# A four-layer transformer kernel on one core: the last net runs three slots earlier against its chunks' attention, and two routing jobs change their place

## The chip, the cores and the metric

The kernel runs on one core of a Trainium2 chip. The metric is device time in microseconds (us), from start to end of one execution. The engines named below are TensorE (PE, with its weight loads as PEld), VectorE (DVE), ScalarE (ACT), GpSimd (POOL) and SyncE (SP, which issues DMAs). Each runs its own instruction queue in order; semaphores order them against each other.

## What is computed

The input is x, 4 sequences of 1024 tokens with 128 features. Four blocks follow, each with a residual and a layer norm behind it:

```python
x = layernorm(x + L0_attn(x))   # causal attention, 16 heads of 64, 2 null keys, cosine scores, ALiBi
x = layernorm(x + L0_ffn(x))    # top-1 of 8 experts, 352 wide, silu-gated
x = layernorm(x + L1_attn(x))   # attention across the 4 sequences, 16 heads of 8, squared-distance scores
x = layernorm(x + L1_ffn(x))    # shared expert + top-2 of 16 experts, all 64 wide, silu-gated; 2x + result
```

In L1_attn the 4 sequences' tokens at one position attend to each other, with weights softmax(-|q_t - q_s|^2 / sqrt(8)). In L1_ffn a sigmoid router picks the two largest of 16 logits per token; ties go to the lower index.

## The kernel before, in words

**First stage: attention turns.** 16 turns t, one for each pair of sequence and head group of four. A turn has 18 steps s (two head pairs times nine key tiles). In each step TensorE forms scores (L635), ACT takes the exponential (L868), POOL cuts the future (L1328), TensorE multiplies by the values one step later (L662), DVE adds up the probabilities (`add`, L1095). In between, jobs that prepare turn n = t + 1 are done at fixed places: the dictionary `AT` gives each its step and "a" (before the values matmuls) or "b" (behind them), `BANK` gives each one of two PSUM banks W. The jobs' order in the dictionary is also the order in which the semaphores count them (`emptied`, `prepared`). A job waits until the previous job in its bank has been emptied (`free_for_prep`). The jobs near the change: R0 and R1 transpose the roots (L545), DVE copies them to RT (L1040); S00 to S13 spread them over the rows (L556), DVE multiplies queries and keys by them (scales, L1049, L1053); E0 and E1 transpose the ALiBi edges, and only where the head group is not "flat". In six turns (t = 5, 6, 9, 10, 13, 14) routing of the first expert layer for tokens that are already done runs alongside: XR transposes the rows (L564), XL forms the logits (L572), DVE picks the expert (`route_pick`, L237 to L245), XK forms ranks (L581 to L585), DVE turns them into row numbers (`route_place`, L1130 to L1140), POOL scatters the rows. In all six the turn prepared is flat, so E0 and E1 are absent. `masses` (L677) and `masses_turned` (L692) form the softmax sums; they use the same banks.

The expert layer (second stage) is not touched.

**Last stage.** 8 chunks of 512 tokens, each with the second attention block and the second expert net. Time is divided into periods u = -1 to 10 of nine slots j = 0 to 8 (`periods`). Each engine has a function `slot(u, j)` that lists what it does there, in order; the slots only order instructions, they have no length of their own. Attention of chunk u stands in period u, with a rest in period u + 1:

- `rows_turned` (j = 0, L1803), `project` (j = 1, L1811), differences, squares, distances, exponentials (j = 2 to 4), `shares` (DVE, j = 5, L2084 to L2089), `weigh` twice (DVE, j = 6 and 7, L2098 to L2106, which ends with `o`), `sums_turned` (j = 8, L1821), which waits for `o`;
- in period u + 1: `form` (j = 0, L1830), `joined` (DVE, L2113) and a norm, `normed_turned` (j = 2, L1840), `route` (j = 3, L1850), sigmoid, `pick_one` and `pick_other` (DVE, j = 4, L2128 to L2137 and L237 to L245), `weights` (DVE, j = 5, L2144 to L2158).

The net of chunk c has nine slots, one for each pair of experts (17 experts of 64, the last slot half full). A net slot is: `gate_up` (PE, G and U, L1870), silu (ACT, L2004), `gated` (DVE, raw = silu(G) * U, L2165), `share` (PE, M, spreads the tokens' expert weights, L1879), `shared` (DVE, hid = raw * M, L2174), and two slots later `down` (PE, Y, L1887). `share` of a slot waits for `shared` of the slot before, since both use the one buffer M. `combine` (PE, L1859) transposes the chunk's weights, ACT copies them (L1997), before the first `share`. At the end `net_home` (ACT, L2010) copies Y, `last_turned` (PE, L1898) transposes it, `ended` (DVE, L2183 and a norm's statistics) adds the residual, POOL takes the root (L183), ACT applies the norm (L194), SP stores the chunk.

Before the change the net of chunk u - 2 stands in period u with net slot i = j, so `combine(u - 2)` is in slot 0 and `last_turned`, `net_home`, `ended` and `norm1.pool_shift` of chunk u - 3 in slot 2, ACT's apply in slot 4.

`form` and `last_turned` write the same PSUM bank (Y1 and T5), `rows_turned`, `combine`, `sums_turned` and `normed_turned` the other one (T and C); `project` uses both.

Of the kernel before, what the change touches and what calls it, by code (L numbers as in the profile page):

```python
# [17 lines left out]
TT = SEQ // P  # L18
# [17 lines left out]
E0, I0 = 8, 352  # L36
# [82 lines left out]
def build(nc, a, out):  # L119
    ctx = ExitStack()  # L120
    with ctx:
# [126 lines left out]
        with ExitStack() as sc:  # L248
# [82 lines left out]
            def probs(p, jt):  # L331
# [4 lines left out]


            AT = {"P00": "0b", "P01": "0b", "P02": "1b", "P03": "2a", "N0": "3b", "T0": "4b", "V3": "4b", "P10": "5a", "P11": "5b",
# [3 lines left out]
            BANK = dict(zip(AT, (0, 1, 1, 0, 0, 0, 1, 1, 0, 1, 0, 1, 0, 0, 1, 0, 1, 1, 0, 0, 1, 0, 1, 0, 1, 0, 0, 1, 0, 0, 1)))  # L342
            PROJ = (("P00", "P01", "P02", "P03"), ("P10", "P11", "P12", "P13"))
            NORMS, TURNED, EDGE, ROOTS = ("N0", "N1"), ("T0", "T1"), ("E0", "E1"), ("R0", "R1")
            VALS = ("V0", "V1", "V2", "V3")
# [120 lines left out]
            def _(pe):  # L466
# [214 lines left out]
                def masses_turned(t, p, ahead):  # L681

                    pe.wait_ge(out_ev[0], stored(t, p, 0, 1))
                    if ahead:
                        k = PREP_BEFORE[p][1]
                        pe.wait_ge(prep_ev[1], emptied(t + 1 + p, k if k in jobs(t + 1 + p) else "V2"))
                    elif p == 0:
                        pe.wait_ge(out_ev[1], stored(t - 1, 1, 1, 3))
                    else:
                        pe.wait_ge(out_ev[1], stored(t, 0, 1, 3))  # L690
                    for u in range(4):
                        last = nc.tensor.transpose(W[1][:, u * P:(u + 1) * P], rows_d[:, u * P:(u + 1) * P], idf[:])  # L692
                    last.then_inc(out_mm, 1)
# [1008 lines left out]
        with ExitStack() as sc:  # L1702
# [62 lines left out]

            LAG = 2
            KS = NJ1 * TT

            def live(c):

                return 0 <= c < TT

            def periods(slot):

# [19 lines left out]
            def _(pe):  # L1796
# [18 lines left out]
                def sums_turned(c):  # L1815

                    pe.wait_ge(o1_ok, 2 * c + 2)
                    pe.wait_ge(qv_ok, c + 1)
                    wait_some(pe, x3_ok, c)
                    for b in range(NB):  # L1820
                        last = nc.tensor.transpose(T[:, b, :], o1[:, b, :], idf[:])  # L1821
                    last.then_inc(o_mm, 1)

                def form(c):

                    pe.wait_ge(ots_ok, c + 1)
                    pe.wait_ge(qv_ok, c + 1)
                    wait_some(pe, lg_ok, c)
                    for b in range(NB):
                        last = nc.tensor.matmul(Y1[:, b, :], ots1[:, b * P:(b + 1) * P], ow1[:], start=True, stop=True)  # L1830
                    last.then_inc(y_mm, 1)
# [21 lines left out]
                def combine(c):  # L1853

                    pe.wait_ge(w3_ok, 3 * c + 3)
                    pe.wait_ge(x3_ok, c + 1)
                    pe.wait_ge(ots_ok, min(c + 2, TT))
                    for b in range(NB):
                        last = nc.tensor.transpose(C[:, b * P:(b + 1) * P],  # L1859
                                                   w3[:, b, :, :].rearrange("p a e -> p (a e)"), idb[:])  # L1860
                    last.then_inc(c_mm, 1)
# [28 lines left out]
                def last_turned(c):  # L1890

                    pe.wait_ge(ys5_ok, c + 1)
                    pe.wait_ge(qv_ok, min(c + 4, TT))
                    pe.wait_ge(yb_ok, min(c + 3, TT))
                    pe.wait_ge(lg_ok, min(c + 2, TT))
                    wait_some(pe, x5_ok, c)
                    for b in range(NB):
                        last = nc.tensor.transpose(T5[:, b, :], ys[:, b * P:(b + 1) * P], idf[:])  # L1898
                    last.then_inc(y5_t, 1)

                def slot(u, j):

                    k = NJ1 * (u - 2) + j
                    if live(u - 2):
                        gate_up(u - 2, j)
                    if j == 0 and live(u - 1):
                        form(u - 1)
                    if j == 0 and live(u - 2):
                        combine(u - 2)
                    if 0 <= k - LAG < KS:  # L1910
                        down(k - LAG)
                    if j == 0 and live(u):
                        rows_turned(u)
                    if live(u - 2):
                        share(u - 2, j)
                    if j == 1 and live(u):
                        project(u)
                    if j == 2 and live(u - 3):
                        last_turned(u - 3)
                    if j == 2 and live(u - 1):  # L1920
                        normed_turned(u - 1)
                    if j == 3 and live(u - 1):
                        route(u - 1)
                    if j == 8 and live(u):
                        sums_turned(u)
# [5 lines left out]
            def _(act):  # L1931
# [80 lines left out]
                def slot(u, j):  # L2012

                    if j == 0 and live(u):
                        rows_normed(u)
                    if j == 2 and live(u - 3):
                        net_home(u - 3)
                    if j == 2 and live(u):
                        queries_values(u)
                    if j == 3 and live(u):  # L2020
                        squares(u)
                    if j == 4 and live(u - 3):
                        norm1.scalar_apply(act, xs, X[:, u - 3], n4(u - 3))
                    if live(u - 2):
                        silu(u - 2, j)
                    if j == 0 and live(u - 2):
                        shares_home(u - 2)
                    if j == 0 and live(u):
                        rows_home(u)
                    if j == 1 and live(u - 1):  # L2030
                        norm2.scalar_apply(act, y2, X[:, u - 1], u - 1)
                    if j == 2 and live(u - 1):
                        normed_home(u - 1)
                    if j == 4 and live(u - 1):
                        sigmoids(u - 1)
                    if j == 4 and live(u):
                        exponentials(u)
                    if j == 8 and live(u):
                        sums_home(u)
# [4 lines left out]
            def _(dve):  # L2044
# [143 lines left out]
                def slot(u, j):  # L2188

                    if j == 1 and live(u):  # L2190
                        own_rows(u)
                    if j == 2 and live(u):
                        differences(u)
                    if j == 3 and live(u):
                        distances(u)
                    if live(u - 2):
                        gated(u - 2, j)
                    if j == 0 and live(u - 1):
                        joined(u - 1)
                    if live(u - 2):  # L2200
                        shared(u - 2, j)
                    if j == 2 and live(u - 3):
                        ended(u - 3)
                    if j == 3 and live(u - 1):
                        logits(u - 1)
                    if j == 3 and live(u + 1):
                        arrive(u + 1)
                    if j == 4 and live(u - 1):
                        pick_one(u - 1)
                        pick_other(u - 1)  # L2210
                    if j == 5 and live(u - 1):
                        weights(u - 1)
                    if j == 5 and live(u):
                        shares(u)
                    if j in (6, 7) and live(u):
                        weigh(u, j - 6)
# [9 lines left out]
            def _(pool):  # L2226
# [7 lines left out]
                def slot(u, j):  # L2234

                    if j == 0 and live(u - 1):
                        norm2.pool_shift(pool, u - 1)
                    if j == 2 and live(u - 3):
                        norm1.pool_shift(pool, n4(u - 3))
                    if j == 3 and live(u + 1):  # L2240
                        norm.pool_shift(pool, n2(u + 1))
                        if u < 0:
                            get_chunk(1)
                        if live(u + 3):
                            get_chunk(u + 3)
# [78 lines left out]
```

## Time and profile before

| | us |
|---|---|
| median of 3 runs | 1722.08 (1718.21 to 1733.55) |
| the profiled execution | 1720.87, its span 1719.2 |
| the last stage, from the first gather of rows (1351.5) | 367.7 |

```profile
span 1719.2 us, 26245 instructions
## 1 busy us (share of the span) xinstructions
PE 1524.1 (89%) x8079; PEld 704.2 (41%) x8079; DVE 1022.5 (59%) x2227; ACT 767.5 (45%) x1425; POOL 533.0 (31%) x589
## 2 busy tenths in 40 slices
PE   4899999999999999999999999998399439999997
DVE  6455555655566664666555576565433267788774
PEclk8899899999999999998899999989599759999999
```

The 40 slices are 43 us each; a digit is the busy share in tenths. TensorE is busy nearly everywhere but at the start, around the change from the first to the second stage (slice 29) and between the expert layer and the last net (slices 32 and 33), where PEclk, the clock that it was granted, is also low. DVE is busiest in the last stage.

### The profile page before, as it was taken

What the parts mean: (1) busy time and instruction counts of PE and PEld (TensorE: products, weight loads), DVE (VectorE), ACT (ScalarE), POOL (GpSimd) and SP (SyncE); (2) the same over time, 40 slices, a digit from 0 to 9 for tenths busy, and PEclk for the clock granted to TensorE, in tenths of its full rate; (3) what the DMA queues carried; (4) which work ended last, traced back from release to release, by engine and by line L of the source; (5) the groups of instructions that cost most, each with busy time, mean ns of one, the idle gap of its engine ahead of it and who ended that gap; (6) DMA issues with size and microseconds to landing.
All of it is one profiled execution on the core that took longest, in us unless ns stands there. A gap on an engine that the chain in (4) does not pass through costs nothing. (4 is left out here: it accounts for less than half of the span.)

```text
span 1719.2 us, 26245 instructions
## 1 busy us (share of the span) xinstructions
PE 1524.1 (89%) x8079; PEld 704.2 (41%) x8079; DVE 1022.5 (59%) x2227; ACT 767.5 (45%) x1425; POOL 533.0 (31%) x589
## 2 busy tenths in 40 slices
PE   4899999999999999999999999998399439999997
PEld 2343344444444344443443434344277324444432
DVE  6455555655566664666555576565433267788774
ACT  3445454454544554544354454544044224444432
POOL 2043341533534444244353424432200321111000
PEclk8899899999999999998899999989599759999999
DMA  3503030320202202022020200000411100000000
GB/s 113 180 1 94 7 100 1 113 71 1 71 6 73 90 1 71 1 71 73 5 77 1 72 13 1 10 2 6 164 52 55 34 12 7 13 13 13 7 6 13
DMA packets 106708, 73.73 MB, mean 43 GB/s; under 512 B 5249, under 2 KB 100761, under 8 KB 106318
## 3 DMA queue, kind: packets, MB, share of 16 engines
q1 hardware_dynamic: 104526, 67.85, 13.1%
q0 software_dynamic: 2048, 4.20, 0.8%
q8 instruction: 71, 1.16, 0.3%
q14 instruction: 63, 0.52, 0.1%
HBM read 24.32 MB, written 47.71 MB: 42 GB/s over the span
## 5 line engine op out<-in xcount | busy, mean ns | idle before, releaser
L868 ACT ACTIVATE P<-S,keyb 128x258 f32<-128x258 f32 (+10 forms) x572 | 305.6, 592 | 401.5 <-PE S L635 294.3
L635 PE MATMUL S<-QT,KT 64*128 64x512 f32 (+5 forms) x1792 | 370.1, 494 | 7.1 <-DVE KT L1053 5.6
L1328 POOL TENSOR_SCALAR_AFFINE_SELECT P<-P 128x256 f32<-128x256 f32 (+1 forms) x256 | 162.0, 633 | 494.3 <-ACT P L868 493.6
L1095 DVE TENSOR_TENSOR Psum<-Psum,P 128x1796 f32<-128x1796 f32 (+7 forms) x256 | 283.1, 1106 | 43.6 <-POOL P L1328 30.5
L662 PE MATMUL O<-P,V 128*64 128x512 f32 (+5 forms) x1536 | 263.7, 448 | 4.5 <-POOL P L1328 3.9
L635 PEld LDWEIGHTS S<-QT,KT 64*128 64x128 f32 (+1 forms) x1792 | 161.0, 185 | 231.2 <-issue 227.3
L1305 POOL TENSOR_TENSOR rn<-nm,half 128x8 f32<-128x8 f32 (+1 forms) x120 | 220.6, 1842 | 90.7 <-DVE R L1008 47.3
L496 PE MATMUL W<-xT,wts 128*128 128x512 f32 x256 | 142.1, 650 | 10.1 <-DVE QT L1049 6.8
L662 PEld LDWEIGHTS O<-P,V 128*64 128x64 f32 (+1 forms) x1536 | 82.0, 139 | 113.9 <-issue 100.2
L1162 DVE TENSOR_TENSOR part<-W,rden 128x512 f32<-128x512 f32 x128 | 82.5, 686 | 77.1 <-PE W L711 76.1
L868 ACT ACTIVATE Psum<-S,keyb 128x1024 f32<-128x1024 f32 (+5 forms) x84 | 70.9, 911 | 125.9 <-issue 64.2
L183 POOL TENSOR_TENSOR norm_rstd<-norm_vareps,half 128x4 f32<-128x4 f32 x24 | 24.9, 1038 | 286.0 <-DVE norm_vareps L174 286.0
L802 ACT COPY qkraw<-W 128x512 f32<-128x512 f32 x128 | 75.3, 589 | 44.7 <-PE W L496 44.3
L2004 ACT ACTIVATE sg<-G 128x512 f32<-128x512 f32 (+1 forms) x72 | 42.9, 596 | 110.9 <-PE U L1870 110.8
L813 ACT ACTIVATE sq<-qkraw 128x512 f32<-128x512 f32 x128 | 80.7, 630 | 14.4
L1049 DVE SCALAR_TENSOR_TENSOR QT<-qkraw,scl,W 128x512 f32<-128x512 f32 x64 | 47.7, 745 | 58.9 <-PE W L556 58.9
L1870 PE MATMUL G<-XT,gw 128*128 128x512 f32 x144 | 81.7, 650 | 0.0
L991 DVE COPY V<-W 128x512 f32<-128x512 f32 x64 | 43.9, 687 | 61.3 <-PE W L524 61.0
L711 PE MATMUL W<-wo,OT 64*128 64x128 f32 x1024 | 73.3, 283 | 7.8 <-DVE rows_n L948 3.4
L1870 PE MATMUL U<-XT,uw 128*128 128x512 f32 x144 | 79.2, 634 | 0.0
L2165 DVE TENSOR_TENSOR raw<-sg,U 128x512 f32<-128x512 f32 (+1 forms) x72 | 49.2, 683 | 49.2 <-ACT sg L2004 49.1
L1887 PE MATMUL Y<-hid,dw 128*128 128x512 f32 x144 | 77.6, 621 | 0.0
(263 smaller groups left out, 2006.7 us busy)
## 6 DMA issues: line engine op xcount, KB each, us to landing
xg<-zero SPq DMA_DIRECT2D x16, 1216.0 KB, 10.3
yg<-zero SPq DMA_DIRECT2D x16, 1216.0 KB, 9.3
wts<-in_w_qkv SPq DMA_DIRECT2D x16, 384.0 KB, 4.1
gu<-in_gu SPq DMA_DIRECT2D x1, 2816.0 KB
xb<-xg SPq DMA_DIRECT2D x40, 64.0 KB, 1.8
yg<-yb SPq DMA_DIRECT2D x40, 64.0 KB, 1.6
X<-in_x SPq DMA_DIRECT2D x4, 512.0 KB, 5.5
wo<-in_w_out SPq DMA_DIRECT2D x16, 128.0 KB, 2.4
```

The lines of the kernel that those rows point to most:

```text
L496: nc.tensor.matmul(W[BANK[k]][:], wt[:, r, at:at + P], xT[:, n // NG % 2, NNULL + 512 * c:NNULL + 512 * c + 512], start=True, stop=True).t ...
L635: last = nc.tensor.matmul(S[hh][0:m, at + c:at + c + w], KT[d, r, p, jt * P:jt * P + m], QT[d, r, p, Q0[jt] + c:Q0[jt] + c + w], start=Tru ...
L662: last = nc.tensor.matmul(O[hh * DH:(hh + 1) * DH, lo:hi], V[0:m, r, jt, (2 * p + hh) * DH:(2 * p + hh + 1) * DH], probs(p, jt)[0:m, hh, l ...
L802: nc.scalar.copy(raw[:, c, j, :], W[BANK[k]][:]).then_inc(prep_ev[BANK[k]], 1)
L813: nc.scalar.activation(sq[:, j, :], raw[:, c, j, :], ACT.Square).then_inc(sq_ok, 1)
L868: last = nc.scalar.activation(probs(p, jt)[0:m, hh, lo:hi], S[hh][0:m, at + lo:at + hi], ACT.Exp, bias=keyb[0:m, r, col:col + 1])
L1095: nc.vector.tensor_tensor(x, x, probs(p, jt)[0:m, :, 0:NQ[jt]], ALU.add).then_inc(add_ok, 1)
L1162: nc.vector.tensor_tensor(part[:, half_, hh], W[hh][:].rearrange("p (u d) -> p u d", u=4), rden[:, p, :, 2 * half_ + hh].unsqueeze(2).broa ...
L1305: nc.gpsimd.tensor_tensor(rn[:, c, u, 0:w], nm[:, c, u, 0:w], powers[:, 0:w], ALU.pow).then_inc(rn_ok, 1)
L1328: nc.gpsimd.affine_select(own, own, [[0, 2], [1, w]], ALU.is_ge, 0.0, base=NNULL if jt == 0 else 0, channel_multiplier=-1).then_inc(cut, 1)
L1870: last = nc.tensor.matmul(o[k % 2][0:n, :], w[:, j * P:j * P + n], XT[:, c % 2, :], start=True, stop=True)
L1887: nc.tensor.matmul(Y[:], dw1[0:ROWS[j], j, :], hid[0:ROWS[j], k % 3, :], start=j == 0, stop=j == NJ1 - 1).then_inc(dn5, 1)
```

## The change

In the last stage a constant `LEAD = 3` and a function `net_slot` place the net: in slot (u, j) now stands net slot i of chunk n, with n and i the quotient and rest of 9(u - 2) + j + 3 by 9. So slots 6 to 8 of period u hold net slots 0 to 2 of chunk u - 1, and slots 0 to 5 hold net slots 3 to 8 of chunk u - 2. `combine` and its copy go with net slot 0, to (u, 6). `last_turned`, `net_home`, `ended` and `norm1.pool_shift` of chunk u - 2 go to (u, 8), ACT's apply of that norm to (u + 1, 1). On DVE `weights` of slot 5 moves ahead of that slot's `gated` and `shared`. Several waits get new operands or are new, because the buffers' users now follow each other in another order (`sums_turned` for `c_ok`, `form` for `x5_ok`, `combine` for `x2_ok`). No instruction of computation is added or removed.

In the attention turns XL moves from 14a to 10b, with bank 1 in place of 0, and XK from 15b to 14b, also with bank 1. `masses_turned` waits for the last job in its bank, which may now be XL.

```diff
-                  "R0": "11a", "S00": "12b", "S01": "12b", "S02": "13b", "S03": "13b", "XL": "14a", "E1": "14b",
-                  "R1": "15a", "XK": "15b", "S10": "16a", "S11": "16b", "S12": "18a", "S13": "18a"}
+            ... "E0": "10b", "XL": "10b",
+                  "R0": "11a", "S00": "12b", "S01": "12b", "S02": "13b", "S03": "13b", "E1": "14b", "XK": "14b",
+                  "R1": "15a", "S10": "16a", "S11": "16b", "S12": "18a", "S13": "18a"}
...
                     if ahead:
-                        k = PREP_BEFORE[p][1]
-                        pe.wait_ge(prep_ev[1], emptied(t + 1 + p, k if k in jobs(t + 1 + p) else "V2"))
+                        n = t + 1 + p
+                        k = next(j for j in ("XL", "E0", "V2") if j in jobs(n)) if p == 0 else PREP_BEFORE[p][1]
+                        pe.wait_ge(prep_ev[1], emptied(n, k))
...
+            LAG, LEAD = 2, 3
+            def net_slot(u, j):
+                return divmod(NJ1 * (u - 2) + j + LEAD, NJ1)
...
 sums_turned:
+                    wait_some(pe, c_ok, c)
 form:
+                    wait_some(pe, x5_ok, c - 1)
 combine:
-                    pe.wait_ge(ots_ok, min(c + 2, TT))
+                    pe.wait_ge(ots_ok, c + 1)
+                    pe.wait_ge(x2_ok, min(c + 2, TT))
 last_turned:
-                    pe.wait_ge(qv_ok, min(c + 4, TT))
-                    pe.wait_ge(yb_ok, min(c + 3, TT))
+                    pe.wait_ge(qv_ok, min(c + 3, TT))
+                    pe.wait_ge(yb_ok, min(c + 2, TT))
...
 TensorE, slot(u, j):
-                    k = NJ1 * (u - 2) + j
-                    if live(u - 2):
-                        gate_up(u - 2, j)
+                    n, i = net_slot(u, j)
+                    k = NJ1 * n + i
+                    if live(n):
+                        gate_up(n, i)
                     if j == 0 and live(u - 1):
                         form(u - 1)
-                    if j == 0 and live(u - 2):
-                        combine(u - 2)
+                    if i == 0 and live(n):
+                        combine(n)
                     if 0 <= k - LAG < KS:
                         down(k - LAG)
...
-                    if live(u - 2):
-                        share(u - 2, j)
+                    if live(n):
+                        share(n, i)
...
-                    if j == 2 and live(u - 3):
-                        last_turned(u - 3)
+                    if j == 8 and live(u - 2):
+                        last_turned(u - 2)
...
 ScalarE:
-                    if j == 2 and live(u - 3):
-                        net_home(u - 3)
+                    if j == 8 and live(u - 2):
+                        net_home(u - 2)
...
-                    if j == 4 and live(u - 3):
+                    if j == 1 and live(u - 3):
                         norm1.scalar_apply(act, xs, X[:, u - 3], n4(u - 3))
...
 VectorE:
+                    if j == 5 and live(u - 1):
+                        weights(u - 1)
+                    if live(n):
+                        gated(n, i)
...
-                    if j == 2 and live(u - 3):
-                        ended(u - 3)
+                    if j == 8 and live(u - 2):
+                        ended(u - 2)
...
-                    if j == 5 and live(u - 1):
-                        weights(u - 1)
...
 GpSimd:
-                    if j == 2 and live(u - 3):
-                        norm1.pool_shift(pool, n4(u - 3))
+                    if j == 8 and live(u - 2):
+                        norm1.pool_shift(pool, n4(u - 2))
```

## Rows read from the trace of the kernel before

**Rows 1.** Windows, one period each from `sums_turned`: us, busy per engine, clock, DMA

```profile
1411.36:1450.51 39.15, 34.25 (x100) 15.57 (x100) 28.68 (x77) 17.36 (x33) 6.35 (x8) 0.94 0.03 7
1450.51:1490.44 39.93, 35.71 (x107) 16.16 (x108) 31.59 (x90) 18.19 (x37) 7.53 (x10) 0.96 0.05 14
...
1568.52:1606.72 38.20, 34.03 (x108) 15.31 (x108) 31.55 (x90) 18.08 (x37) 3.68 (x6) 1.00 0.02 8
...
1646.61:1678.70 32.09, 31.73 (x96) 13.29 (x96) 21.87 (x65) 13.63 (x24) 2.42 (x4) 1.00 0.02 9
```

**Rows 2.** Waits of TensorE in the last stage: total us, times, longest

```profile
PE W L1821 <- DVE o L2106: 35.8, 8, 15.0
```

**Rows 3.** Timeline of TensorE, period 6: start, us, instruction, [idle before <- releaser]

```profile
1571.71 0.41 PE L1859 MATMUL W<-idb,w 128*51 128x128 bf16 x4
...
1581.86 0.66 PE L1898 MATMUL W<-idf,ys 128*128 128x128 f32 x4
...
1589.77 1.13 PE L1870 MATMUL G<-XT,gw 128*128 128x512 f32 x2
...
1592.86 1.13 PE L1870 MATMUL G<-XT,gw 128*128 128x512 f32 x2
...
1595.89 0.39 PE L1879 MATMUL M<-comb,sel 51*128 51x512 bf16 x1 [0.19 <-DVE hid L2174]
...
1600.76 0.39 PE L1879 MATMUL M<-comb,sel 51*128 51x512 bf16 x1 [1.71 <-DVE hid L2174]
...
1606.72 0.66 PE L1821 MATMUL W<-idf,o 128*128 128x128 f32 x4 [1.93 <-DVE o L2106]
```

**Rows 4.** Timeline of DVE, the same period

```profile
1571.85 0.69 DVE L2165 TENSOR_TENSOR raw<-sg,U 128x512 f32<-128x512 f32 x1 [2.09 <-ACT sg L2004]
...
1582.75 0.68 DVE L2183 SCALAR_TENSOR_TENSOR xs<-X,W 128x512 f32<-128x512 f32 x1
...
1590.90 0.19 DVE L2128 TENSOR_SCALAR sc<-sc 128x64 f32<-128x64 f32 x1
...
1594.43 0.68 DVE L2165 TENSOR_TENSOR raw<-sg,U 128x512 f32<-128x512 f32 x1
...
1597.65 0.20 DVE L2155 CAST w<-wt 128x68 bf16<-128x68 f32 x1
...
1606.24 0.42 DVE L2106 TENSOR_TENSOR o<-prod 128x256 f32<-128x256 f32 x1
```

**Rows 5.** Timeline at the start of the last stage, all engines

```profile
1393.79 0.59 ACT L1984 COPY XT<-W 128x512 f32<-128x512 f32 x1 [1.22 <-PE W L1840]
...
1404.59 0.22 DVE L2155 CAST w<-wt 128x68 bf16<-128x68 f32 x1
...
1410.88 0.42 DVE L2106 TENSOR_TENSOR o<-prod 128x256 f32<-128x256 f32 x1
...
1412.26 1.91 PE L1870 MATMUL G<-XT,gw 128*128 128x512 f32 x2
```

**Rows 6.** Timeline of DVE in period 8: the last pick, the last weight

```profile
1670.21 0.22 DVE L245 TENSOR_TENSOR hot<-key,top 128x64 f32<-128x64 f32 x1
...
1673.58 0.20 DVE L2155 CAST w<-wt 128x68 bf16<-128x68 f32 x1
```

**Rows 7.** Timelines of attention turns: turn 5 with routing, then turn 2 without

```profile
480.93 1.06 PE L572 MATMUL W<-rw,xtr 128*128 128x8 f32 x8
485.68 0.39 PE L545 MATMUL W<-idb,R 128*24 128x128 bf16 x4 [1.93 <-DVEq L1121]
487.42 0.19 PE L581 MATMUL W<-rhot,tri 128*128 128x32 bf16 x1 [0.55 <-DVE RT L1040]
...
488.16 0.17 DVE L1130 TENSOR_TENSOR rspot<-W,held 128x32 f32<-128x32 f32 x1
...
488.74 0.19 DVE L1140 TENSOR_REDUCE place<-rspot 128x4 uint32<-128x32 f32 x1
...
269.83 0.87 PE L662 MATMUL O<-P,V 128*64 128x386 f32 x4 [0.35 <-POOL P L1328]
272.86 0.50 PE L556 MATMUL W<-RT,selr 24*128 24x512 bf16 x1 [1.73 <-DVE RT L1040]
```

More of the change, by code:

```diff
@@ L338, in build @@
             AT = {"P00": "0b", "P01": "0b", "P02": "1b", "P03": "2a", "N0": "3b", "T0": "4b", "V3": "4b", "P10": "5a", "P11": "5b",
[3 rows of a table removed]
-            BANK = dict(zip(AT, (0, 1, 1, 0, 0, 0, 1, 1, 0, 1, 0, 1, 0, 0, 1, 0, 1, 1, 0, 0, 1, 0, 1, 0, 1, 0, 0, 1, 0, 0, 1)))
[3 rows of a table added]
+            BANK = dict(zip(AT, (0, 1, 1, 0, 0, 0, 1, 1, 0, 1, 0, 1, 0, 0, 1, 0, 1, 1, 1, 0, 0, 1, 0, 1, 1, 1, 0, 1, 0, 0, 1)))
             PROJ = (("P00", "P01", "P02", "P03"), ("P10", "P11", "P12", "P13"))
@@ L1763, in build @@
                 s4("x_ok5"), s4("m5"), s4("st_out"))
-            LAG = 2
+            LAG, LEAD = 2, 3
             KS = NJ1 * TT
@@ L2015, in slot @@
                         rows_normed(u)
-                    if j == 2 and live(u - 3):
-                        net_home(u - 3)
+                    n, i = net_slot(u, j)
+                    if j == 8 and live(u - 2):
+                        net_home(u - 2)
                     if j == 2 and live(u):
@@ L2021, in slot @@
                         squares(u)
-                    if j == 4 and live(u - 3):
+                    if j == 1 and live(u - 3):
                         norm1.scalar_apply(act, xs, X[:, u - 3], n4(u - 3))
[L2024 to L2027, printed above, removed]
+                    if live(n):
+                        silu(n, i)
+                    if i == 0 and live(n):
+                        shares_home(n)
                     if j == 0 and live(u):
@@ L2195, in slot @@
                         distances(u)
-                    if live(u - 2):
-                        gated(u - 2, j)
+                    n, i = net_slot(u, j)
+                    if j == 5 and live(u - 1):
+                        weights(u - 1)
+                    if live(n):
+                        gated(n, i)
                     if j == 0 and live(u - 1):
                         joined(u - 1)
-                    if live(u - 2):
-                        shared(u - 2, j)
-                    if j == 2 and live(u - 3):
-                        ended(u - 3)
+                    if live(n):
+                        shared(n, i)
+                    if j == 8 and live(u - 2):
+                        ended(u - 2)
                     if j == 3 and live(u - 1):
```

2 rows, old and new, of the table AT are left out of this document.

## Prediction

> **What bounds the kernel now.** I read the table of windows over the last stage first. From one period to the next (39.15, 39.93 and 38.20 us in the rows, the others like them) TensorE is busy 34 of 38.20 us at full clock, so it is the bound, with about 4 us of holes per period; DVE is busy 31.55 of them, so it is close behind [rows 1]. Period 8, which has no attention, and the net of chunk 7 behind it have no such holes: 31.73 of 32.09 us busy in period 8 [rows 1]. Then the waits: TensorE's largest in this stage is `sums_turned` (L1821), which waits for the attention's last sum `o` on DVE, 35.8 us over 8 times, once 15.0 [rows 2]. The timelines of one period show why. In slots 0 to 4 TensorE runs without a hole; a clean slot takes 1592.86 - 1589.77 = 3.09 us. In slots 5 to 8 it waits 0.19, 1.71 and 1.93 us for DVE (and once more, 0.34, by the same pattern) [rows 3]. DVE has just begun the routing picks (1590.90), then has one slot's pair of products (1594.43), the weights (to 1597.85), the shares and the two `weigh`s, and ends `o` at 1606.66: 15.76 us without a gap [rows 4]. So a period is a TensorE-bound part (slots 0 to 4) and a DVE-bound part (slots 5 to 8).
>
> At the stage's start the net has nothing to do: XT of chunk 0 is there at 1394.4, its weights at 1404.8, yet the first gate matmul of the net begins at 1412.26, at half clock, behind the attention of chunk 1, whose `o` ends at 1411.30 [rows 5]. That hole is the 15.0 us of [rows 2].
>
> **The change, part by part** (against the profiled run: span 1719.2, its time 1720.87; the median of the runs is 1.2 us above that).
>
> *Head.* Net slots 0 to 2 of chunk 0 now stand in slots 6 to 8 of period 1, before `sums_turned(1)`. Gate 0 can run at 1396; `combine`, the copy of its result and share 0 need the weights (1404.8). DVE then has the shares of chunk 1, two pairs of products and two `weigh`s; in a later period this very list takes 1606.66 - 1597.85 = 8.8 us [rows 4], so `o` is ready at 1413.6 at the earliest. TensorE is at half clock: a gate pair takes 2 x 1.71 = 3.4 us (the G row starts 1.71 before its U) [rows 5]. Share 0 ends near 1407.0, gate 1 1410.4, gate 2 1414.2, then one `down` and share 2: `sums_turned(1)` at 1415.6, against 1411.36. Bounds: 1413.6, and 1417.8 if everything up to there is at half clock. Term: +4.2 (+2.2 to +6.4).
>
> *First full period.* Before, it starts cold and takes 39.15 [rows 1]; now it is warm and ordinary, 38.20 - 0.84 (next step) = 37.4. Term: -1.8. The two `down`s that the old period lacked (slots 0 and 1) are in the ordinary period's length.
>
> *Every later period.* `combine` moves from slot 0 to 6, `last_turned` from 2 to 8, out of the part where TensorE is the bound: 0.34 + 0.50 us start to start (durations 0.41 and 0.66 overlap their successors) [rows 3]. The holes in slots 5 to 8 take them. Within those slots nothing shortens: the weights now stand ahead of pair 5, so TensorE's share 6 waits some 2.1 us longer (1597.85 - 1595.75, [rows 4]), but share 7 waited for the same DVE list anyway; DVE's list from picks to `o` is the same 15.76 us. The copy of the weights' turned result (ACT, 0.6) ends before pair 5 does. ACT's norm apply moves from slot 4 to 1, where it must fit between `rows_home` and the silu; by the timeline it does, and at slot 4 the silu waited for TensorE. The DMA issues are the same and stay behind the same signals; SP only gets each output store about three slots earlier, POOL's `pool_shift` goes from behind slot 2 to behind the gathers of slot 3, which wait for nothing there. `ended` (2.3 us, 1582.75 to 1585.1) moves to behind pair 8, queued ahead of pair 0, `joined` and the next norm; DVE idled 2.09 there [rows 4], so about 0.2 us is late, and `joined`'s result is needed four us later. Term: 5 x -0.84 = -4.2; bounds 0 and -4.2.
>
> *Tail.* From `sums_turned(7)` the old kernel needs 1719.2 - 1646.61 = 72.6 us [rows 1]. Removed: three slots, 9.3; one `combine` and one `last_turned`, 0.8; two small waits, 0.4. Added: chunk 7's `combine` now comes in slot 6 of period 8. Old: picks end at 1670.43, pair 5, weights end at 1673.78 [rows 6]; now the weights follow the picks, 1672.5 - 0.84 = 1671.7, while TensorE has ended gate 6 at about 1669.8 and has 1.3 us (`combine`, `down`) to do before share 6, which needs pair 5, ready 1.3 after the weights, 1673.0. Stall 2.1. Term: -9.3 - 0.8 - 0.4 + 2.1 = -8.4 (bounds -6.7, if half clock follows the stall, and -10.5, without it).
>
> *Clock.* Each period holds one stretch at half clock. Where it falls into slots 5 to 8 it costs nothing (38.20), where behind `o` it costs 1.7 us (39.93) [rows 1]; three periods of six pay. The holes move, and I can't tell where the stretches go: 0, bounds -5.1 and +5.1. The first G at 1412.26 is at 1.2 GHz after the 15 us hole [rows 5]. The Trainium skill ("TensorE: Matmul & The Clock Gate", Part 1) says that the array runs at half rate by default and that recent activity releases it; the trace agrees. By that rule alone fewer holes would mean fewer slow stretches, and all of them gone is the first rival below.
>
> *Routing in attention turns* (turns 5, 6, 9, 10, 13, 14; the next turn is flat, so E0 and E1 are absent). XL goes from 14a to 10b and bank 0 to 1, XK from 15b to 14b. Now R1 waits 1.93 us for DVE, whose picks are queued behind two late `add`s, and XK 0.5 more [rows 7]. Both waits vanish. But DVE is the bound there: a turn without routing shows the next wait, the spread of R1's roots behind RT, 1.73 us [rows 7]. XL's 1.0 us of matmuls now stands ahead of the scales that the late `add`s wait for, and so delays both engines alike; `route_place`, 488.93 - 488.16 = 0.77 us, comes ahead of RT on DVE, and XK's 0.3 us ahead of the spread on TensorE. The wait there becomes 1.73 + 0.77 - 0.3 = 2.2 us, and with the 0.35 us for POOL's cut, which that turn also shows, 2.55 us stand against 1.93 + 0.55 = 2.48 now [rows 7]. Term 0. Bounds: -2.5 x 6 = -14.9 if the two waits simply go; +0.77 x 6 = +4.6 if the place comes on top of what routed turns lose now. Nearest the row of the unrouted turn: 0. Queued behind XL's picks on DVE is RT of R0, for which it idles some 3 us. `masses_turned` now waits for those picks, which end before its own turn.
>
> Sum: 4.2 - 1.8 - 4.2 - 8.4 + 0 = -10.2. Profiled run 1710.7; against the median 1711.9. I say 1711.5.
>
> **The rivals.**
> - *Clock*: no slow stretch falls behind `o`: 5.1 less, 1706.5. For it: fewer holes; against: every period now has one stretch, hole or not. 0.15.
> - *Routing waits go*: R1's and XK's 2.48 us in six turns are real gain, 14.9 less, 1696.6. For it: TensorE is the bound over the turn; against: the 1.73 us wait in a turn without any routing. 0.10.
> - *The periods don't shorten*: `ended` and the norm apply, at their new places, hold up pair 0 and the silu of slot 1 as much as TensorE was relieved: terms two and three lose 5 us, 1716.5. For it: DVE's 2.3 us against 2.09 idle; against: only 0.2 is late. 0.14.
> - *Slower than before*: `form` now waits for `ended`'s first operation of the slot before (they share PSUM). That is done 2.05 us behind `o`, `form` comes at 2.27. If it came a whole `ended` later, each of seven boundaries would cost up to 2.3 us: 1711.5 + 16 = 1727.6. It decides from 1.5 us per boundary. Against: `last_turned` stands ahead of `sums_turned` and its input is copied 3 us before. 0.06, with half of it beyond 1% once clock loss is added.
>
> **How the numbers follow.** The forecast has 0.55, with its own range 1706 to 1716.5. The range is 1701 to 1719: it takes in the clock and the third rival and leaves out the routing gain and the slower case. One per cent, about what a measurement can tell here from no change, is 17.2 us. Faster by more needs the routing gain, or clock and the best bounds together: 0.12. Slower by more (over 1739): 0.03. Same: 0.85.
>
> **What would show it.** `sums_turned(1)` about 4 us later, with three gate pairs before it; periods of 37.4 us (39.1 with a slow stretch); TensorE's wait at share 6 near 2 us, and less at L1821, above all the 15.0; in period 8 a 2 us stall at share 6; no wait at R1, and about 1.9 us at the spread behind it, with routed turns as long as before. Periods that stay at 38.2, or waits at `form`, would prove steps three and five wrong; routed turns 2 us shorter, the routing step.

## The result, and the profile after

The changed kernel takes 1714.92 us (median of 15 runs, 1710.36 to 1721.04) against 1724.20 us of the kernel before (15 runs, 1717.11 to 1733.55) on the same chip: ratio 0.9949, 95% interval 0.9935 to 0.9964. That is some 9 us less, within 1%. The forecast was 10.2 less. The size is right, but two of its terms, both put at nothing, were wrong with opposite signs: one by 5 us, the other by 8 to 10, as the parts and the experiments show.

The page of the changed kernel, its span, TensorE's busy share in 40 slices and the clock granted to it:

```profile
span 1717.9 us, 26266 instructions
...
PE   4899999999999999999999999998669748989997
...
PEclk8899998998989999899989999999779958999999
```

This profiled execution took 1719.64 us, 4.7 above its median, and that of before 1720.87, 3.3 below its own. So the two spans differ by only 1.3 us, and the parts must be compared, not the spans:

| part | before | after | difference |
|---|---|---|---|
| to `masses` of turn 0 | 106.5 | 107.8 | +1.3 |
| attention turns, `masses` of turn 0 to that of turn 15 | 1076.4 | 1090.3 | +13.9 |
| from there to the last stage | 168.6 | 169.9 | +1.3 |
| last stage: head, to `sums_turned(1)` | 59.9 | 63.0 | +3.1 |
| first full period | 39.15 | 37.25 | -1.9 |
| five later periods | 196.1 | 186.2 | -9.9 |
| tail, from `sums_turned(7)` | 72.6 | 63.5 | -9.1 |

The last stage is 17.8 us shorter, and the attention turns, where the forecast expected nothing, are 13.9 longer. Of these 13.9, 5.6 lie in turns 0 to 4, whose instructions are the same in both kernels (the table by turns in experiment 4), and so can't come from the change.

Windows of the changed kernel: the head, the first full period and the last of the six, the tail; then the attention turns, and the second half of turn 6. Columns as in [rows 1]; the last three are clock, DMA share and GB/s.

```profile
1368.00:1430.95 62.95, 27.60 (x69) 15.30 (x69) 34.25 (x101) 17.41 (x39) 26.25 (x28) 0.55 0.08 21
1430.95:1468.20 37.25, 34.12 (x108) 15.14 (x108) 29.94 (x79) 16.66 (x33) 6.33 (x8) 1.00 0.03 8
...
1617.18:1654.44 37.26, 35.54 (x110) 15.50 (x108) 29.82 (x79) 18.21 (x37) 2.42 (x4) 0.95 0.02 7
1654.44:1717.90 63.46, 53.13 (x147) 20.68 (x145) 35.07 (x100) 21.05 (x39) 4.83 (x8) 0.95 0.04 13
...
107.84:1198.14 1090.30, 1035.75 (x6091) 448.90 (x6090) 646.54 (x1142) 518.76 (x917) 432.17 (x458) 0.95 0.14 41
...
546.55:582.29 35.74, 32.38 (x196) 13.97 (x195) 23.26 (x43) 13.72 (x24) 12.76 (x16) 0.90 0.01 3
```

The same two stretches of the kernel before:

```profile
106.54:1182.93 1076.39, 1022.01 (x6092) 443.87 (x6091) 647.18 (x1142) 517.70 (x917) 431.94 (x458) 0.96 0.14 41
...
538.44:571.64 33.20, 29.55 (x196) 13.35 (x195) 23.26 (x43) 13.56 (x23) 11.88 (x16) 1.00 0.01 3
```

Two things are to be read here. Every period is now 37.2 us, whether its clock is 1.00 or 0.95, where before it was 38.20 or about 39.9 [rows 1]. And half a turn with the same matmuls went from 33.20 to 35.74 us, while its clock went from 1.00 to 0.90.

The waits of TensorE in the last stage (us in total, times, longest):

```profile
PE W L1827 <- DVE o L2116: 18.7, 6, 12.8
...
PE W L1867 <- DVE w L2165: 11.8, 5, 4.9
PE W L1867 <- issue: 5.1, 3, 1.7
```

`sums_turned` (now L1827) waits 18.7 us where it waited 35.8 [rows 2]. In its place `combine` (now L1867) waits for the weights, 16.9 us in eight times (for three of them, 5.1 us, the profile names no releaser; that they are the weights too is inferred from the place).

One period of TensorE, to be read against [rows 3]; L1878 is `gate_up`:

```profile
1607.05 0.41 PE L1867 MATMUL W<-idb,w 128*51 128x128 bf16 x4 [1.71 <-DVE w L2165]
...
1608.83 2.07 PE L1878 MATMUL G<-XT,gw 128*128 128x512 f32 x2
...
1617.18 0.64 PE L1827 MATMUL W<-idf,o 128*128 128x128 f32 x4
```

And of DVE, to be read against [rows 4]: `ended` (L2193), the next pair of products (L2175), the first pick, the last weight, the last `o`:

```profile
1581.11 0.68 DVE L2193 SCALAR_TENSOR_TENSOR xs<-X,W 128x512 f32<-128x512 f32 x1
1583.36 0.68 DVE L2175 TENSOR_TENSOR raw<-sg,U 128x512 f32<-128x512 f32 x1
...
1601.24 0.20 DVE L2138 TENSOR_SCALAR sc<-sc 128x64 f32<-128x64 f32 x1 [0.16 <-ACT sc L1999]
...
1606.80 0.20 DVE L2165 CAST w<-wt 128x68 bf16<-128x68 f32 x1
...
1616.69 0.42 DVE L2116 TENSOR_TENSOR o<-prod 128x256 f32<-128x256 f32 x1
```

The three holes of 0.19, 1.71 and 1.93 us in slots 5, 6 and 8 have become one of 1.71 us in slot 6, and it stands 10 us ahead of `o`. DVE's list from picks to `o` still takes 15.87 us (15.76 before), which sets the length of slots 5 to 8. The half-clock stretch (a gate of 2.07 us in place of 1.13) lies inside them, so nothing is paid for it.

A routed attention turn of the changed kernel (turn 6), to be read against the first three of [rows 7]: R1 (L545), the first spread S10 (L556), values and scores:

```profile
566.31 0.39 PE L545 MATMUL W<-idb,R 128*24 128x128 bf16 x4
...
570.48 0.37 PE L556 MATMUL W<-RT,selr 24*128 24x512 bf16 x1 [2.42 <-DVE RT L1041]
570.78 0.97 PE L662 MATMUL O<-P,V 128*64 128x258 f32 x4
...
573.31 3.87 PE L635 MATMUL S<-QT,KT 64*128 64x512 f32 x8 [0.28 <-DVE KT L1054]
```

The waits at R1 (1.93) and XK (0.55) are gone, and one of 2.42 stands at the spread, as forecast (2.2). But behind it eight score matmuls take 3.87 us, at half clock, where the same eight of the kernel before take 2.08.

### The profile page after: what moved, and what is told of

Same layout as the page of the kernel before. It is cut to its first block and busy times, and to the rows that moved or that the text cites. A ratio compares the mean times of both kernels' runs of the same rounds, so it can differ in the third digit from the quotient of the medians.

```text
span 1717.9 us, 26266 instructions
## 1 busy us (share of the span) xinstructions
PE 1535.4 (89%) x8079; PEld 706.7 (41%) x8079; DVE 1022.7 (60%) x2227; ACT 769.2 (45%) x1425; POOL 533.1 (31%) x589
## 5 line engine op out<-in xcount | busy, mean ns | idle before, releaser
L635 PE MATMUL S<-QT,KT 64*128 64x512 f32 (+5 forms) x1792 | 378.1, 502 | 6.2 <-DVE KT L1054 4.6
L496 PE MATMUL W<-xT,wts 128*128 128x512 f32 x256 | 150.4, 685 | 8.5 <-DVE QT L1050 5.5
L1878 PE MATMUL G<-XT,gw 128*128 128x512 f32 x144 | 82.3, 655 | 0.0
L556 PE MATMUL W<-RT,selr 24*128 24x512 bf16 x128 | 49.5, 441 | 33.7 <-DVE RT L1041 29.8
L1878 PE MATMUL U<-XT,uw 128*128 128x512 f32 x144 | 76.9, 617 | 0.0
L496 PEld LDWEIGHTS W<-xT,wts 128*128 128x128 f32 x256 | 43.3, 204 | 79.5 <-issue 51.8
```

Of the source, the lines that this page charges most:

```text
L496: nc.tensor.matmul(W[BANK[k]][:], wt[:, r, at:at + P], xT[:, n // NG % 2, NNULL + 512 * c:NNULL + 512 * c + 512], start=True, stop=True).t ...
L635: last = nc.tensor.matmul(S[hh][0:m, at + c:at + c + w], KT[d, r, p, jt * P:jt * P + m], QT[d, r, p, Q0[jt] + c:Q0[jt] + c + w], start=Tru ...
L1878: last = nc.tensor.matmul(o[k % 2][0:n, :], w[:, j * P:j * P + n], XT[:, c % 2, :], start=True, stop=True)
```

## The experiments

Each was run against the kernel before on the chip that it ran on; these were three chips, with medians of the kernel before from 1722.84 to 1723.88 us. Theory H ("half clock"): the attention turns are longer only because more of them runs at 1.2 GHz. Its rival R: the routing jobs' new place costs TensorE or DVE time in itself.

**1. Only the net, only the routing.** The first leaves `AT`, `BANK` and `masses_turned` as before the change, the second changes nothing else.

> The changed kernel with the attention turns' XL and XK put back where they were. The change's profile shows the last stage 17.8 us shorter and the attention turns 15 us longer than before. Theory A (the attention turns' length is set by where the half-clock stretches fall, and the routing jobs' place has nothing to do with it): same time as the whole change, about 0.995 of the kernel before, with a last stage of about 350 us. Theory B (the routing jobs' new place costs the turns what the net gains): about 0.990, 17 us less than before, and attention turns as long as before.

Measured: 1705.43 us (1704.44 to 1706.86), ratio 0.9895 (0.9877 to 0.9913), 17.4 less than before.

> The kernel before with only the routing jobs moved. Theory A: the same time as before, 0.998 to 1.002, with S10's spread waiting 2.4 us in place of R1's 1.93 and XK's 0.55. Theory B: 8 to 15 us more than before, 1.005 to 1.009. The rival of the prediction (the two waits go): 15 us less, 0.991.

Measured: 1730.69 us (1725.13 to 1736.14), ratio 1.0047 (1.0030 to 1.0063), 7.9 more. So the net's part alone gains 1%, and the routing's part loses about half of that; the two add up to 9.5 us less, where the whole change measured 9.3. Windows, net only (the turns, then the last stage's first full period):

```profile
107.28:1186.08 1078.80, 1024.33 (x6091) 445.18 (x6090) 646.62 (x1142) 518.03 (x917) 432.56 (x458) 0.96 0.14 41
...
1417.62:1454.87 37.25, 34.12 (x108) 15.14 (x108) 29.93 (x79) 16.67 (x33) 6.34 (x8) 1.00 0.03 8
```

and routing only:

```profile
107.13:1192.16 1085.03, 1029.83 (x6091) 447.19 (x6090) 646.28 (x1142) 518.77 (x917) 430.68 (x458) 0.96 0.14 41
```

The gain lies in the last stage (350.3 us, with the periods of the whole change), the loss in the turns.

**2. Which of the two moves.** XL moves to 10b as in the change, XK stays at 15b with bank 0:

```diff
-  "XL": "10b" ... "XK": "14b", "R1": "15a"
+  "XL": "10b" ... "R1": "15a", "XK": "15b"
```

> The kernel before with XL and its picks at 10b, but XK and route_place where they were (15b, behind RT on DVE). If route_place ahead of RT is what lengthens the hole from 1.7 to 2.4 us and brings the half-clock stretches: about the time before (0.997 to 1.001), with 1.6 us of waiting at S10's spread or XK in place of 2.42. If XL's work ahead of the late adds does it: as the routing-only kernel, 1.0047.

Measured: 1733.10 us (1727.77 to 1740.07), ratio 1.0058 (1.0035 to 1.0081), 10.0 more. XL's move alone is enough to bring the whole loss. XK then waits 2.06 us itself, and the half-clock stretch comes again:

```profile
490.82 0.19 PE L581 MATMUL W<-rhot,tri 128*128 128x32 bf16 x1 [2.06 <-DVE RT L1041]
...
494.07 4.00 PE L635 MATMUL S<-QT,KT 64*128 64x512 f32 x8 [0.28 <-DVE KT L1054]
```

**3. Filling the hole.** The net's change alone, and TensorE does matmuls whose result nobody reads (the bank is overwritten next) where it would wait for the second roots: ahead of R1 in routed turns, ahead of S10 in the others.

```diff
+                def fill(n, alone):
+                    if alone: return
+                    pe.wait_ge(prep_ev[1], emptied(n, "S03"))
+                    for _ in range(6):
+                        nc.tensor.matmul(W[1][:], idb[:], GK[:, 0:512], start=True, stop=True)
```

> As the net-only kernel, with six bf16 matmuls of 512 columns, whose result is overwritten unread, in the hole of each attention turn behind step 14 (before R1's transposes in turns with routing, before S10's spread in the others), into a PSUM bank that the next spread overwrites. If the half-clock stretches of the turns come from that hole of 1.7 to 1.9 us: fewer of them (the changed kernel's profile has 109 us of them between 130 and 1170 us, the one before 78), and up to half of that, 30 us and more, off the time. If they come from elsewhere, the same time or 0.9 us per turn more (the fill at half clock is longer than the hole).

Measured: 1683.71 us (1678.48 to 1685.61), ratio 0.9759 (0.9736 to 0.9782), 21.7 less than the net alone. This is the fastest kernel of the study. Windows, the turns and the second half of turn 6:

```profile
106.81:1161.55 1054.74, 1016.71 (x6181) 444.62 (x6181) 646.05 (x1142) 517.36 (x917) 429.23 (x458) 0.99 0.14 42
...
531.20:564.40 33.20, 30.96 (x202) 13.86 (x200) 23.26 (x43) 14.47 (x24) 9.30 (x14) 1.00 0.01 3
```

The place in an unrouted turn, TensorE's timeline:

```profile
266.52 1.47 PE L544 MATMUL W<-GK,idb 128*128 128x512 bf16 x6
...
268.23 0.38 PE L568 MATMUL W<-RT,selr 24*128 24x512 bf16 x1 [0.24 <-DVE RT L1052]
```

Before, TensorE waited 1.73 us there [rows 7]; now it works 1.47 and waits 0.24. Adding 90 matmuls made the kernel 21.7 us faster, and the turns' clock went from 0.96 to 0.99.

With nine in place of six:

> As the kernel with the old places of the routing jobs and the fill, with nine filling matmuls in place of six: 2.2 us where the hole is 1.7 to 1.9. If the clock is what counts, the remaining half-clock stretches (three turns) go, worth up to 7 us, against 0.3 to 0.5 us more of work in each of 15 turns: 1677 to 1690. If six were enough and the rest is chance: 5 us more, 1688.

Measured: 1684.46 us (1682.33 to 1685.54), ratio 0.9774 (0.9752 to 0.9796): no better. The turns take 1055.3 us although only 7 us of them are at half clock. The nine take 2.12 us in a hole of 1.73, so the three more matmuls outlast it.

**4. The whole change, filled.** The same `fill` in the changed kernel, ahead of XK in routed turns:

> The whole change with the six filling matmuls: before XK's matmuls in turns with routing (the bank that S10 would offer is in use there), before S10's spread in the others. With the routing jobs in their old place and the same fill the kernel took 1683.7 us. If the 8 us that the new place costs without the fill are clock alone (the hole of 2.42 us in one piece brings a half-clock stretch in each of these turns): within 2 us of 1683.7. If route_place ahead of RT is a cost in itself, the bound of the prediction: 0.8 us for each of six turns, 1688.5.

Measured: 1686.38 us (1680.43 to 1690.93), ratio 0.9779 (0.9753 to 0.9804); the interval overlaps that of the net alone with the filling. The 2.7 us between them lie between the two expectations (2 or less, and 4.8), so the total alone doesn't decide. The turns, and the second half of turn 6, with the routing's new place and no half clock:

```profile
108.59:1168.56 1059.97, 1020.91 (x6182) 446.17 (x6181) 645.77 (x1142) 517.75 (x917) 436.13 (x458) 0.99 0.14 42
...
530.27:563.43 33.16, 30.69 (x201) 13.91 (x201) 23.23 (x43) 13.57 (x23) 13.11 (x16) 1.00 0.01 3
```

33.16 us with the new place, 33.20 with the old (kernel before, and experiment 3): the place costs nothing in this half turn at full clock. That speaks against R. The filling in the six routed turns alone:

> The whole change, with the six filling matmuls only in the six turns with routing (before XK). The routing jobs' new place cost 8 us without a fill. If that cost is the half-clock stretches of these six turns (48 us of them in the change's profile): up to 24 us off 1714.9, so about 1695, with the other nine turns as before. If the cost sits in the other turns or in the jobs themselves: 1710 or more.

Measured: 1700.93 us (1698.03 to 1705.26), ratio 0.9871 (0.9848 to 0.9895), 13.4 us less than the unfilled change by the two ratios. The expectation had the other nine turns as before; they were not. This table gives the sum of the second halves of the turns, where all of the half clock is (the first halves take 557.9 to 558.0 us in all seven kernels):

| kernel | turns 0 to 4, us | six routed turns, us | turns 7, 8, 11 and 12, us |
|---|---|---|---|
| before | 169.7 | 214.1 | 134.6 |
| net only | 171.5 | 210.8 | 138.5 |
| net only, `last_turned` back (experiment 5) | 174.1 | 210.8 | 138.5 |
| routing only | 169.7 | 216.3 | 141.1 |
| XL only | 172.3 | 214.9 | 142.0 |
| changed | 175.3 | 215.0 | 142.1 |
| changed, routed turns filled | 174.3 | 204.8 | 132.8 |

Without a filling, the last two columns together are 348.7 to 349.3 us with the old place and 356.9 to 357.4 with the new one: 8 us, the loss that the experiments measured. Much of it lies not in the turns whose jobs moved but in the four unrouted turns between and behind them, whose instructions are the same; the filling of the routed turns takes 9.3 us off these four as well. Turns 0 to 4, before the first routed one, scatter by 5.6 us without any cause in the code.

The windows of all half turns give one more test of H. The time at half clock is worked out from each half turn's length and clock, as length x 2 x (1 - clock), and summed over the 15 turns of the windows above (the clock has two digits, so a sum is good to some 2 us):

| kernel | routing's place | turns, us | at half clock, us | turns - 0.36 x that |
|---|---|---|---|---|
| before | old | 1076.4 | 78 | 1048 |
| net only | old | 1078.8 | 82 | 1049 |
| routing only | new | 1085.0 | 97 | 1050 |
| XL only | XL new | 1087.0 | 105 | 1049 |
| changed | new | 1090.3 | 111 | 1050 |
| changed, routed turns filled | new | 1069.8 | 54 | 1050 |
| changed, filled | new | 1060.0 | 27 | 1050 |
| net only, filled | old | 1054.7 | 15 | 1049 |

The 0.36 is from net only and net only, filled: 24.1 us shorter for 66.7 us less at half clock. With this one price all eight kernels come to 1048 to 1050. (The kernel with nine matmuls would come to 1053: there the filling itself costs.) The three unfilled kernels with XL's new place have 97 to 111 us at half clock, the five unfilled ones with the old place (those of experiments 5 to 7 among them) 75 to 88. At most 1 to 3 us can be the place itself: TensorE's waits for the roots add up to 28.8 us in the changed kernel's turns against 26.7 before (14.0 + 11.6 + 1.1).

These are single executions, but the clock of every execution is on record. Its median over the whole program is 0.929 before (17 runs; 19 on the other chip), 0.9235 for routing only (12) and 0.921 for XL only (8), which makes 244, 265 and 274 us at half clock. With the same 0.36 all three come to 1635 us. So H carries nearly all of the loss.

**5. Where the last stage's gain comes from.** The net alone, with `last_turned`, `ended`, `pool_shift` and the norm's apply back at their old slots, and their old waits:

```diff
-                    if j == 8 and live(u - 2):
-                        last_turned(u - 2)
+                    if j == 2 and live(u - 3):
+                        last_turned(u - 3)
```

> As the net-only kernel, but last_turned, ended and the norm behind them stay in slot 2 (ACT's apply in slot 4) of the period after, as before. If the step is right that moving last_turned out of slots 0 to 4 gives 0.5 us per period, periods of 37.75 instead of 37.25 us and about 2.5 us more over five periods, and another 0.5 in period 8. If the periods' length is set by DVE alone, nothing.

Measured: 1712.66 us (1707.52 to 1714.58), ratio 0.9930 (0.9910 to 0.9950), 7.2 more than the net alone. The stage takes 355.4 us against 350.3: later periods of 37.7 to 38.0 in place of 37.25 (the first, which has no `last_turned`, stays at 37.24), and a tail of 65.6 in place of 63.5; the rest of the 7.2 lies in the turns (88 us at half clock in this execution), in turns 0 to 4 by the table above, and so isn't the edit's. TensorE's timeline, `combine`, which waits as in the net alone:

```profile
1561.46 0.41 PE L1865 MATMUL W<-idb,w 128*51 128x128 bf16 x4 [1.77 <-DVE w L2163]
```

The place of `last_turned` is worth 0.4 to 0.7 us a period; the forecast had 0.50.

**6. The order of the weights.** The net alone, with DVE's `weights` behind slot 5's products, where they stood before the change:

```diff
-                    if j == 5 and live(u - 1):
-                        weights(u - 1)
                     if live(n):
                         gated(n, i)
...
+                    if j == 5 and live(u - 1):
+                        weights(u - 1)
```

> As the net-only kernel (1705.4 us), but DVE's weights stand behind slot 5's pair of products, as before the change. By the prediction's list DVE needs the same 15.8 us in each period, so the periods stay at 37.25; combine comes 1.35 us later. In period 8, where nothing but the chain to combine counts, the stall of 1.7 us becomes 3.1: 1.4 us more in all, 1706.8. If the order is essential (share 6 then waits for both), 1 us more per period, 1713.

Measured: 1718.28 us (1714.83 to 1726.81), ratio 0.9983 (0.9965 to 1.0002), 12.9 more than the net alone: far more than the pair of products (1.3 us) by which `combine` was expected later, and above both expectations. Periods take 38.3, two of them 39.8 and 40.0. TensorE's timeline:

```profile
1561.36 0.41 PE L1866 MATMUL W<-idb,w 128*51 128x128 bf16 x4 [2.89 <-DVE w L2164]
```

and DVE's, with the M that it needs (L1886), a little later:

```profile
1563.63 0.60 PE L1886 MATMUL M<-comb,sel 51*128 51x512 bf16 x1
1564.33 0.69 DVE L2183 TENSOR_TENSOR hid<-raw,M 128x512 f32<-128x512 f32 x1 [0.89 <-DVE raw L2174]
```

`combine` waits 2.89 us in place of 1.71, so M comes later than DVE is ready for it: it ends at 1564.23, and DVE, which bounds this part, idles 0.89. Late on TensorE has become late on the bounding engine. The matmuls between `combine` and M run at half clock here (2.01 us where the changed kernel takes 1.13), so part of the 0.89 is clock, and the two longest periods have a clock of 0.91: stretches cost again. The two causes were not separated. The six periods take 233.1 us in all, 2.1 less than before the change, where the net alone has 223.5; the tail (64.6) keeps most of its gain.

**7. One slot more.** The net alone with `LEAD = 4`, `net_home` at slot 7:

> The net-only kernel (1705.4 us) with the net one slot earlier still: LEAD = 4, combine in slot 5, net_home in slot 7, the rest in place. If three slots is where the weights are just in time: combine now waits some 3 us longer for them with less work behind it to make up; from the run with the weights behind slot 5's pair (1.1 us per period for 1.2 us later weights) I expect 1 to 2 us more in each of seven periods, against 3.1 us less in the tail that the stall there takes back: 1710 to 1722. If earlier is simply better: 1702.

Measured: 1736.68 us (1732.07 to 1741.15), ratio 1.0084 (1.0063 to 1.0106), 31 more than the net alone. `combine` now stands so early that it waits for the weights 4.74 us, TensorE's timeline:

```profile
1567.94 0.63 PE L1866 MATMUL W<-idb,w 128*51 128x128 bf16 x4 [4.74 <-DVE w L2164]
```

and DVE idles for it:

```profile
1570.51 0.60 PE L1886 MATMUL M<-comb,sel 51*128 51x512 bf16 x1
1571.20 0.69 DVE L2183 TENSOR_TENSOR hid<-raw,M 128x512 f32<-128x512 f32 x1 [2.72 <-issue]
```

Periods take 41.0 to 41.5 us, each at a clock of 0.92. The time is 15 us above the longest that was expected. Three slots are not a mid-point of a slope: one more is 4 us a period worse, the lost clock included.

**8. Keeping the clock up in the head.** Experiment 3's kernel, and 13 more matmuls without use ahead of gate 0, at (1, 2) and ahead of the first `combine`:

> The net-only kernel with the fill of six in the turns (1683.7 us), and fills in the holes at the start of the last stage as well: nine fp32 matmuls of 512 columns (into Y, which is overwritten later) in the 12.8 us hole before sums_turned(0), one before slot 2 of period 1, three before the first combine. If half clock is what makes the head 63 us: the matmuls on the chain to the weights of chunk 0 halve (2.9 us), and of the 3.1 us that the gates of slots 7 and 8 add some 1.3 go: 4 us less, 1679.5. If DVE's list alone sets the head: same time.

Measured: 1686.91 us (1680.53 to 1689.12), ratio 0.9777 (0.9752 to 0.9802): not better than without, and not the 1679.5 that clock in the head would have given. The head is 1.2 us shorter, the first full period 1.7 longer. TensorE's timeline:

```profile
1366.18 1.11 PE L1838 MATMUL W<-idf,o 128*128 128x128 f32 x4 [4.46 <-DVE o L2138]
...
1397.63 0.66 PE L1838 MATMUL W<-idf,o 128*128 128x128 f32 x4 [1.94 <-DVE o L2138]
1399.06 1.91 PE L1889 MATMUL U<-XT,uw 128*128 128x512 f32 x2
```

A hole of 4.46 us that I had left brings half clock back (1.11 us for what takes 0.66), and behind `sums_turned(1)`, which now waits 1.94, a new stretch begins where TensorE is the bound.

## Why the prediction was right, and where it was wrong

**Head, +4.2: +3.1.** The mechanism was right, but for the engine that ends last. Gates 0 to 2, `combine` and the first shares come before `sums_turned(1)`. In TensorE's timeline of the changed kernel gates 1 and 2 (L1878) show that the clock rose within gate 2 (1.49 us for a G where half clock takes 2.08), earlier than the term assumed. So TensorE was not the last, as the term had it: `sums_turned(1)` waits 0.47 for `o`, and DVE's list set the time:

```profile
1420.89 0.63 PE L1867 MATMUL W<-idb,w 128*51 128x128 bf16 x4 [4.94 <-DVE w L2165]
...
1422.72 2.08 PE L1878 MATMUL G<-XT,gw 128*128 128x512 f32 x2
...
1426.97 1.49 PE L1878 MATMUL G<-XT,gw 128*128 128x512 f32 x2
...
1430.95 0.66 PE L1827 MATMUL W<-idf,o 128*128 128x128 f32 x4 [0.47 <-DVE o L2116]
...
1679.38 0.41 PE L1867 MATMUL W<-idb,w 128*51 128x128 bf16 x4 [1.71 <-DVE w L2165]
```

**First full period, -1.8: -1.9.** Right.

**Later periods, -0.84 each: -0.95 each.** Right (38.20 to 37.25), and experiment 5 confirms the share of `last_turned`; that of `combine` (0.34) was not tested alone. Wrong in place: the wait for the weights stands at `combine`, 1.71 us, and not at share 6. `combine` is the first that needs them, which the step overlooked, without harm to the sum.

**Tail, -8.4: -9.1.** Right. The stall in period 8 is 1.71 us (last row above), not 2.1.

**Clock in the periods, 0: -5.1.** The failed term of the last stage. Three of six periods paid 1.7 us; now none does. The term had named this as its bound. The rival had it for 0.15. The reason against it, that every period has a stretch, was misread: the very period of 38.20 in [rows 1] has a clock of 1.00. Nor was it a reason: in the changed kernel two periods have one (clock 0.95) and take the same 37.25. With one hole in slot 6, well ahead of `o`, a stretch has room to end inside DVE's part; that this is why none costs is argued from the timelines. The net only and the filled kernels show the same 37.25, with a clock of 1.00 in nearly all periods, so fewer stretches came as well. Where the holes stand elsewhere, in experiments 6 and 7 and in the first period of experiment 8, stretches cost again.

**Routing in attention turns, 0: +8 to +10.** The failed term of the first stage. "Both waits vanish" and "the wait there becomes 2.2 us, and 2.55 stand against 2.48" were right: 2.42 us, and 33.16 against 33.20 us for the half turn at full clock. What failed is the step from equal holes to equal time. It had bounds from waits alone (-14.9 and +4.6) and left the clock out, though the term next to it had priced a stretch in a period. With the new place 97 to 111 us of the turns are at half clock, not 75 to 88. Experiments 3 and 4 show that the price goes through the clock. Why this pattern brings more stretches is not settled, and the added time is largely in unrouted turns, where no hole was moved. One longer hole in place of two is an argument only; no run kept the place and changed the hole's length alone.

**The rivals.** "Routing waits go" fell: the waits moved to the spread. "The periods don't shorten" fell: `ended` is followed by the next products without a gap (1581.11, 1583.36). "Slower, because `form` waits for `ended`" fell: `form` waits once in the whole stage, 0.7 us for its own input, as before. That the total came out near 1711.5 is luck: the net gained 7 us more than forecast (17.4 against 10.2), and the routing lost 8 to 10 that the forecast had at nothing.

## What to carry to other kernels

When a change moves holes on TensorE, price the clock with the hole: read the clock of the stretch behind it, in every stage that the change touches, and in the parts of the stage that it does not touch. Compare parts that are the same in both kernels first: they show how much a single profiled execution scatters. Put a hole that can't be closed early in a part that another engine bounds, and fill one in a dense part with matmuls without use, no longer than the hole. When work is moved ahead, ask where its first consumer's input is made: one slot too far (`LEAD = 4`) or one operation out of order (`weights`) makes the bounding engine wait and costs more than the move gains.

## What the hardware showed that was not expected

The prediction counted half clock in the last stage and gave it no price in the attention turns. Here 7 to 10% of these turns ran at 1.2 GHz although TensorE was busy for 95% of them, and none of its waits there was longer than 1.9 us before the change or 2.8 after. Second halves of turns, which have these holes, have up to some 10 us at half clock, and some with the same work have none (33.20 us at a clock of 1.00 against 35.74 at 0.90 for turn 6). By the estimate of experiment 4 the turns lost 0.36 us for each us at half clock: 28 us in the kernel before (0.36 x 78), which no view of waits shows. 1.47 us of matmuls in a hole of 1.7 took most of it away. What happened in one turn also changed the clock of the next: with only the routed turns filled, the unfilled ones between and behind them got shorter by 9.3 us.

The Trainium skill ("TensorE: Matmul & The Clock Gate", section "A second HAM failure mode: psum-queue depth-cycling") says that short idle times between groups of matmuls can make the clock swing between its two levels. These traces agree: in the turns the clock changed between 2.4 and 1.2 GHz with no wait of TensorE above 2.8 us, and 78 to 111 us of some 1080 were at 1.2. The skill says this of another kernel.
